# A five-layer hybrid block on one core: the layers behind the attention run in two halves of the tokens, woven into each other, and the attention loop is unrolled

## The chip, the cores and the metric

The kernel runs on one core of one Trainium2 chip. A core has five engines that run at the same time, each with its own queue of instructions: TensorE (PE in the profile, its weight loads PEld), VectorE (DVE), ScalarE (ACT), GpSimd (POOL) and SyncE (SP), which here only starts DMAs. Every queue is executed in order: an instruction that waits on a semaphore holds up all that stands behind it on its engine. The metric is the device time in microseconds of one execution.

## The reference

The input is 8 images of 64 channels and 16x16 pixels, 2048 tokens of 64 channels behind the convolutions. All is float32. Abridged:

```python
x = conv_attention(x)              # L0: non-local block on pooled keys, batch norm
x = binary_conv(x)                 # L1: 3x3 and 1x1 convolutions of signs
x = x + attention8(layernorm(x))   # L2: 8 heads per image, softmax over 256 tokens
n = layernorm(x)
x = x + sum_e gate2[e] * (gelu(n @ W1[e] + b1[e]) @ W2[e] + b2[e])       # 8 experts
x = x + haar_attention(layernorm(x), W_Q, pinv(W_Q), W_V, W_O)          # L3
n = layernorm(x)
x = x + sum_e gate3[e] * ((silu(n @ w1[e]) * (n @ w2[e])) @ w3[e])       # 16 experts
```

The gates are a softmax over the experts of which only the two largest count. The Haar attention has rotary queries and keys, their norms, scores against block sums, a variance-scaled softmax, and value sums by block. The pseudo-inverse of W_Q is found by a Newton iteration of 24 steps, whose small matrix products are run between those of the L2 attention.

## The kernel before

**Tokens and tiles.** The tokens stand as 16 tiles of 128 (`T`, 128 partitions by 16 by 64), the stream that the layers add to. For the experts the normed tokens are turned and split into a high and a low part (`XS`), 4 chunks of 512 tokens. The engines' programs are written out by hand, one block each, and tied by counted semaphores.

**Front.** L0 and L1, then `layer_norm(0)` on VectorE over all 16 tiles (`bn_stats` per tile, small operations, a square root on ScalarE, `tensor_tensor` multiplications at L1495, `split_low` at L375), the transposes in `ln_pe` and `split_high` on ScalarE.

**Attention.** `attention_steps` runs 36 steps on each engine, a pair of heads each, software-pipelined over five engines; 24 of them (3 rounds of 8) stand in a hardware loop, `Fori`. In those 24 steps TensorE also does the Newton products (`newton_a` L887, `newton_b` L891 and L892, tiles of 64x64), VectorE `newton_y` and `newton_x`, and GpSimd `newton_z`. GpSimd scales each block of probabilities (L494). Once per round of the loop VectorE copies the Newton factors (L1567).

**Behind the attention, all 16 tiles at once.** `layer_norm(1)`, the gate logits (L793), `gate(0)`, then the gates are transposed (L804), copied to `gT` (L578), stored to DRAM, and loaded back as rows that all partitions share (L428, L437). The first expert layer is 32 chunks (8 experts by 4 chunks): two `hidden` products, a gelu (L713), the multiplication by the gate row on VectorE (L1622), an `output` product. Meanwhile GpSimd has split the weights of the second expert layer (`split_weights`, L450 and L452), then it is idle. Next the sums are turned back (L1188), `layer_norm(2)`, the Haar attention (`l3_pe`, `l3_vector`, `l3_pool`), `layer_norm(3)`, gate logits, `gate(1)`, and the way through DRAM again.

**Last layer.** 64 chunks (16 experts by 4): four `hidden` products (L999) into a pair of PSUM banks (three pairs in turn), silu on ScalarE (L721), the product of the two halves on VectorE (L1639), the multiplication by the gate row on GpSimd (L548), an `output` product (L1007, two instructions each). `hidden` runs six chunks ahead of `output`; eight `hid` buffers.

## Time and profile before

| | us |
|---|---|
| median of 3 runs | 449.83 (449.23 to 450.18) |
| profiled execution, whole time | 450.27 |
| its span, first to last instruction | 448.3 |
| start to the end of L1 | 0 to 50.4 |
| first norm | 50.4 to 61.8 |
| attention | 61.8 to 211.5 |
| norm, gates, gate rows | 211.5 to 243.8 |
| first expert layer (32 chunks) | 243.8 to 278.5 |
| turn, norm, Haar attention, norm, gates, gate rows | 278.5 to 347.9 |
| last expert layer (64 chunks) and store | 347.9 to 448.3 |

All steps below are placed in the profiled execution's span; some 2.0 us of its time lie outside the span.

### The profile page before, as it was taken

The page shows a single profiled execution, that of the slowest core. Times are in us where ns is not written, and L with a number is a line of the kernel's source. Part 1 is how long each engine was busy: PE and PEld are TensorE (multiplying, and loading weights), DVE is VectorE, ACT ScalarE, POOL GpSimd, SP SyncE. Part 2 cuts the span into 40 slices and gives each one's busy share as a digit, 9 for nine tenths or more (in the row PEclk, how much of TensorE's full clock was granted, in tenths as well). Part 3 has the DMA queues.
Part 4 walks back from the last instruction along what each step waited for, and adds up shares of the span by engine and source line. Part 5 has one row for each costly group of instructions (what it writes and reads, how often), then busy time and mean ns, then how long its engine had stood idle before and what let it go on. Part 6 is the DMA issues. An engine that isn't in the chain of part 4 may idle for free.

```text
span 448.3 us, 6934 instructions
## 1 busy us (share of the span) xinstructions
PE 369.8 (83%) x2147; PEld 237.7 (53%) x2147; DVE 292.5 (65%) x691; ACT 219.0 (49%) x545; POOL 191.2 (43%) x186
## 2 busy tenths in 40 slices
PE   4577279999999999997394999763476899999996
PEld 1462166777777777775271344532264355555552
DVE  2857967777787777774962565998994144444443
ACT  1434267777777777784341455532145233434332
POOL 4300035544555455452850000050100888888885
PEclk9867559999999999999656899867588899999999
DMA  7805000000000000000005980000002855444421
GB/s 230 172 0 189 0 0 2 1 2 2 0 0 0 0 0 0 0 2 1 1 0 174 320 258 4 1 0 2 0 1 76 311 187 188 153 164 155 187 94 48
DMA packets 16698, 32.81 MB, mean 73 GB/s; under 512 B 5728, under 2 KB 9504, under 8 KB 16672
## 3 DMA queue, kind: packets, MB, share of 16 engines
q1 hardware_dynamic: 16672, 32.49, 22.3%
q8 instruction: 13, 0.21, 0.2%
q14 instruction: 13, 0.11, 0.1%
HBM read 31.76 MB, written 0.72 MB: 72 GB/s over the span
## 4 chain that ended last, share of the span: by engine, by line
PE 62%; DVE 21%; ACT 7%; issue 5%; DMA 2%; POOL 1%; POOLq 0%; SPq 0%; DVEq 0%; ACTq 0%
PE ps L999 13%; PE ps L1007 7%; PE ps L843 7%; PE ps L854 6%; PE ps L870 6%; PE ps L958 4%; PE ps L950 3%; DVE xn L1495 2%; ACT va_vb L607 2%; DVE ln L1477 2%; DVE XS L375 2%; PE ps L819 1%; PE ps L820 1%; DVE negmax L1547 1%; PE ps L891 1%
## 5 line engine op out<-in xcount | busy, mean ns | idle before, releaser
L494 POOL TENSOR_TENSOR va_vb<-va_vb,rowinv 128x512 f32<-128x512 f32 x64 | 67.1, 1049 | 74.4 <-DVE rowinv L1554 74.4
L999 PE MATMUL ps<-XS,w3hl 128*128 128x512 f32 x256 | 70.0, 417 | 0.7 <-ACT gT L578 0.7
L721 ACT ACTIVATE wy<-ps 128x512 f32<-128x512 f32 x64 | 38.2, 598 | 63.8 <-PE ps L999 63.8
L999 PEld LDWEIGHTS ps<-XS,w3hl 128*128 128x128 f32 x256 | 47.1, 194 | 34.5 <-DVE hid_more L1639 5.7
L607 ACT ACTIVATE va_vb<-ps,negmax 128x256 f32<-128x256 f32 x128 | 59.5, 472 | 10.7 <-DVE negmax L1547 10.3
L1547 DVE TENSOR_REDUCE negmax<-ps 128x2 f32<-128x512 f32 x64 | 44.1, 689 | 10.0 <-PE ps L843 9.0
L843 PE MATMUL ps<-keys_gates,xcur 128*128 128x256 f32 x256 | 48.0, 311 | 2.2 <-DVE keys_gates L1539 2.2
L458 POOL TENSOR_TENSOR xn<-T,lnc 128x512 f32<-128x512 f32 x4 | 4.2, 1042 | 101.3 <-DVE lnc L1485 101.3
L843 PEld LDWEIGHTS ps<-keys_gates,xcur 128*128 128x128 f32 x256 | 35.7, 195 | 14.7 <-issue 8.1
L854 PE MATMUL ps<-consts,va_vb 128*128 128x128 f32 x256 | 40.5, 280 | 2.8 <-POOL va_vb L494 2.4
L870 PE MATMUL ps<-pT,vproj 128*64 128x256 f32 x256 | 34.5, 392 | 0.0
L854 PEld LDWEIGHTS ps<-consts,va_vb 128*128 128x128 f32 x256 | 28.5, 142 | 9.2 <-POOL va_vb L494 4.5
L598 ACT ACTIVATE keys_gates<-ps 128x512 fp32r<-128x512 f32 x32 | 19.1, 598 | 26.9 <-PE ps L820 26.7
L607 ACT ACTIVATION_READ_ACCUMULATOR va_vb<-ps,negmax 128x1 f32 x128 | 25.7, 201 | 0.0
L1639 DVE TENSOR_TENSOR hid_more<-ps,wy 128x512 f32<-128x512 f32 x16 | 11.1, 692 | 20.6 <-ACT wy L721 20.6
L1539 DVE TENSOR_TENSOR keys_gates<-ps,keys_gates 128x512 fp32r<-128x512 f32 x32 | 21.9, 685 | 1.5 <-ACT keys_gates L598 1.4
L591 DVE COPY pT<-ps 128x512 f32<-128x512 f32 x32 | 21.6, 675 | 1.9 <-PE ps L854 1.9
L950 PE MATMUL ps<-XS,w2hl 128*128 128x512 f32 x64 | 22.3, 480 | 0.0
L780 PE MATMUL ps<-consts,xn 128*128 128x128 f32 x32 | 7.6, 369 | 17.4 <-DVE xn L1495 17.4
L1639 DVE TENSOR_TENSOR hid_g<-ps,wy 128x512 f32<-128x512 f32 x16 | 11.1, 692 | 14.8 <-ACT wy L721 14.8
L950 PEld LDWEIGHTS ps<-XS,w2hl 128*128 128x128 f32 x64 | 12.9, 222 | 14.2 <-issue 3.2
L1554 DVE RECIPROCAL rowinv<-rowsum 128x2 f32<-128x2 f32 x64 | 10.5, 165 | 15.1 <-ACT va_vb L607 14.4
(305 smaller groups left out, 749.0 us busy)
## 6 DMA issues: line engine op xcount, KB each, us to landing
pT<-gates_row SPq DMA_DIRECT2D x18, 512.0 KB, 4.7
vproj<-gates_row SPq DMA_DIRECT2D x16, 512.0 KB, 4.8
gate_row_keys<-gates_row SPq DMA_DIRECT2D x14, 512.0 KB, 4.7
early<-in_f_in SPq DMA_DIRECT2D x1, 2048.0 KB, 8.9
consts<-in_consts SPq DMA_DIRECT2D x1, 816.0 KB, 5.5
x<-in_x SPq DMA_DIRECT2D x1, 512.0 KB, 3.7
w2raw<-in_f_in SPq DMA_DIRECT2D x1, 512.0 KB, 3.8
out<-in_f_out SPq DMA_DIRECT2D x1, 512.0 KB
```

Source lines behind the costliest of these rows:

```text
L494: gp.tensor_tensor(prob[:, n % 4], prob[:, n % 4], rowinv[:, n % 4, :].unsqueeze(2).broadcast_to([P, U, N]), ALU.mult).then_inc(S("p_scale ...
L607: ins = act.activation(prob[:, n % 4, u, :], ps[:, 1 + n % 2, u * N:(u + 1) * N], ACT.Exp, bias=negmax[:, n % 4, u:u + 1], accum_out=rowsu ...
L721: act.activation(act_out[:, kk % 2, :], ps[:, 2 * (kk % 3), :], ACT.Silu).then_inc(S("f3_act"), 1)
L843: mm = pe.matmul(ps[:, 1 + n % 2, u * N:(u + 1) * N], xcur[:, g, u * P:(u + 1) * P], K[:, k % 2, n % 2, :], start=(part == 0), stop=(part ...
L854: mm = pe.transpose(ps[:, 3 + n % 2, su * N + u * P:su * N + (u + 1) * P], prob[:, n % 4, u, su * P:(su + 1) * P], ident)
L870: mm = pe.matmul(ps[h * C:(h + 1) * C, 5, 0:N], vproj[:, g, su, head * C:(head + 1) * C], pT[:, (2 * k + h) % 4, su, :], start=(k % 4 == 0 ...
L950: mm = pe.matmul(ps[:, kk % 4, :], w2hl[:, s, e], XS[:, c * CHUNK:(c + 1) * CHUNK], start=(s == 0), stop=(s == 1))
L999: mm = pe.matmul(ps[:, 2 * (kk % 3) + w, :], w3hl[:, s, e, w * HID:(w + 1) * HID], XS[:, c * CHUNK:(c + 1) * CHUNK], start=(s == 0), stop= ...
L1007: pe.matmul(ps[half, bank, :], out3[:, e, :], hid[kk % 8], start=False, stop=False, skip_group_check=True).then_inc(S("f3_out_chunk"), 1)
L1539: tt(KL[:, k % 2].rearrange("p h n -> p (h n)"), ps[:, 0, :], KH[:, k % 2].rearrange("p h n -> p (h n)").bitcast(F32), ALU.subtract).then_ ...
L1547: dve.tensor_reduce(negmax[:, n % 4, :], ps[:, 1 + n % 2, :].rearrange("p (u n) -> p u n", u=U), AX.X, ALU.max, negate=True).then_inc(S("m ...
L1639: tt(hid[kk % 8], ps[:, 2 * (kk % 3) + 1, :], act_out[:, kk % 2, :], ALU.mult).then_inc(S("f3_glu"), 1)
```

## The change

The order of the work behind the attention and the shares of the engines are new; the arithmetic is that of before, but for Newton's scale factors.

- Norms, gates and Haar attention take half the tokens (8 tiles) at a time. `NORMS` gives their order: norm 0 of both halves, norm 1 of both, then norms 2 and 3 of half 0, then 2 and 3 of half 1.
- `in_turn` and `chain_first` interleave two generators in each engine's program: a main one with a yield per chunk (per pair for TensorE, two yields) and a chain one. The Haar attention, norm 3 and gates of half 0 are woven into the first expert layer's half 1; those of half 1 into the last layer's half 0. The last layer's half 1 stands alone.
- Norm 0 of half 1 is done inside the first attention steps; norm 1 and the gates of half 0 inside the last ones; norm 1 and the gates of half 1 inside the first expert layer's half 0.
- GpSimd now multiplies by the gate rows in both expert layers; it splits the last layer's weights in 32 pieces, one in each of the first 32 attention steps.
- The attention is unrolled; Newton's copies of factors are gone; its products are 128 by 128 wide (`nsX` and `nsY` doubled).
- The norm's subtraction and multiplication are one `tensor_scalar` per tile. The copies of V3 move from VectorE to ScalarE. PSUM for hidden products is five single banks in turn (before: four banks, and three pairs), so that bank 5 is the Haar attention's.
- `keep_clock` (20 filler products on TensorE) is no longer called. Gate rows lie in eight slots of half the tokens.

```diff
+        def in_turn(main, chain, lead=0):
+            for k, _ in enumerate(main):
+                if k >= lead:
+                    next(chain, None)
+            for _ in chain:
+                pass
+        def chain_first(main, chain):
+            next(chain, None)
+            for _ in main:
+                next(chain, None)
+            for _ in chain:
+                pass
...
-            for k in range(-2, 2):
-                step(0, k, lambda pair: pair >= 0)
-            with eng.Fori(0, J - 1) as j:
...
+            for k in range(-2, STEPS + 2):
+                step(0, k, lambda pair: 0 <= pair < STEPS)
+                if beside:
+                    beside(k)
...
 # GpSimd
+        def weigh_pool(gp, which, h):
+            for k in range(2 * EXPERTS[which]):
+                K = 2 * EXPERTS[which] * h + k
+                slot, filled = row_of(which, h, k // 2)
+                gp.wait_ge(S(f"gate_row{slot}"), 16 * filled)
+                gp.wait_ge(S(("f2_act", "f3_glu")[which - 2]), K + 1)
+                gp.tensor_tensor(hid[K % 8], hid[K % 8], gate_rows[slot][:, k % 2 * CHUNK:(k % 2 + 1) * CHUNK],
+                                 ALU.mult).then_inc(S(f"f{which}_hid_ready"), 1)
+                yield
...
+            for _ in weigh_pool(gp, 2, 0):
+                pass
+            in_turn(weigh_pool(gp, 2, 1), chain_pool(gp, 0), lead=2)
+            in_turn(weigh_pool(gp, 3, 0), chain_pool(gp, 1), lead=5)
+            for _ in weigh_pool(gp, 3, 1):
+                pass
...
 # ScalarE
+            gT_act(act, 2, 0)
+            in_turn(gelu_act(act, 0), second_norm_act(act))
+            sums_act(act, 0)
+            ln_act(act, 2, 0, ACT.Gelu)
+            ln_high_act(act, 2, 0)
+            in_turn(gelu_act(act, 1), chain_act(act, 0, ACT.Gelu), lead=2)
+            sums_act(act, 1)
+            ln_act(act, 2, 1, ACT.Silu)
+            ln_high_act(act, 2, 1)
+            in_turn(silu_act(act, 0), chain_act(act, 1, ACT.Silu), lead=5)
+            for h in range(2):
+                if h == 1:
+                    for _ in silu_act(act, 1):
+                        pass
+                act.wait_ge(S("f3_out_chunk"), 2 * EXP3 * (h + 1))
+                act.activation(yfin[:, h, :], ps[:, 6 + h, :], ACT.Copy).then_inc(S("out_ready"), 1)
...
 # ScalarE, in chain_act
+            act.wait_ge(S("a_var_ready"), h + 1)
+            act.activation(s9[:, 3], s9[:, 2], ACT.Sqrt).then_inc(S("a_std_ready"), 1)
+            act.preload_act_table((ACT.Exp, table)[h])
+            yield
+            act.wait_ge(S("z_ready"), h + 1)
+            act.activation(e9[:], z9[:], ACT.Exp).then_inc(S("e9_ready"), 1)
+            act.preload_act_table((ACT.Sqrt, table)[h])
...
 # TensorE
+            gates_pe(pe, 2, 0)
+            in_turn(ffn2_pe(pe, 0), second_norm_pe(pe))
+            second = ffn2_pe(pe, 1)
+            next(second)
+            turn_pe(pe, 0)
+            ln_pe(pe, 2, 0)
+            chain_first(second, chain_pe(pe, 0))
+            pe.wait_ge(S("w3_split"), EXP3)
+            third = ffn3_pe(pe, 0)
+            next(third)
+            turn_pe(pe, 1)
+            ln_pe(pe, 2, 1)
+            chain_first(third, chain_pe(pe, 1))
+            for _ in ffn3_pe(pe, 1):
+                pass
...
+            def newton_a(s):
+                pe.wait_ge(S("nsx_ready"), s + 2)
+                pe.matmul(ps[:, 6, 0:C], as_weights(nsAT[:]), nsX[:, 2, :], start=True,
+                           stop=True).then_inc(S("ns_ax"), 1)
...
 # VectorE
+                for q in range(tiles.start, tiles.stop):
+                    ins = ts(xn[:, q, :], T[:, q, :], lnc[:, 1, q:q + 1], lnc[:, 7, q:q + 1], ALU.subtract, ALU.mult)
...
+            def chain(h):
+                for _ in range(4):
+                    yield
+                yield from l3_vector(dve, h, step, tt, ts, stt)
+                yield from layer_norm(3, h)
+                yield
+                yield from gate(3, h)
+            def products(h):
+                for k in range(2 * EXP3):
+                    K = 2 * EXP3 * h + k
+                    dve.wait_ge(S("f3_act"), K + 1)
+                    if K >= 8:
+                        dve.wait_ge(S("f3_out_chunk"), K - 7)
+                    tt(hid[K % 8], ps[:, (2 * K + 1) % 5, :], act_out[:, K % 2, :],
+                       ALU.mult).then_inc(S("f3_glu"), 1)
+                    yield
...
+            for h in range(2):
+                turn(h)
+                for _ in layer_norm(2, h):
+                    pass
+                if h == 0:
+                    for _ in chain(0):
+                        pass
+            in_turn(products(0), chain(1), lead=5)
+            for _ in products(1):
+                pass
```

`l3_vector` now has a yield behind each of its parts: squares' sums; two cosine products; rotation, norms and scaled basis; diagonal scores; scale; far scores; variance; standardised scores; exponentials' sums; diagonal weights; prefix part. `layer_norm` has four, `gate` two.

## Rows read from the trace of the kernel before

**Rows 1.** The page, busy time of each engine over the span (microseconds, share, instructions)
```profile
PE 369.8 (83%) x2147; PEld 237.7 (53%) x2147; DVE 292.5 (65%) x691; ACT 219.0 (49%) x545; POOL 191.2 (43%) x186
```

**Rows 2.** Busy time by stage: stretch, its length, engines' busy time, granted clock, DMA
```profile
50.40:61.80 11.40, 3.19 (x12) 2.45 (x12) 10.73 (x39) 5.13 (x11) 3.59 (x3) 0.50 0.00 0
61.80:211.50 149.70, 146.39 (x1102) 112.27 (x1102) 109.28 (x257) 108.33 (x344) 73.07 (x88) 0.98 0.00 1
211.50:243.80 32.30, 18.70 (x140) 13.40 (x140) 20.00 (x63) 10.86 (x21) 15.43 (x9) 0.63 0.11 31
243.80:278.50 34.70, 33.86 (x117) 13.24 (x118) 20.79 (x33) 17.16 (x27) 0.00 (x0) 0.90 0.66 216
278.50:288.10 9.60, 6.94 (x36) 3.43 (x36) 8.53 (x34) 3.51 (x7) 1.04 (x1) 1.00 0.01 2
288.10:323.00 34.90, 17.17 (x129) 11.21 (x129) 31.18 (x65) 10.59 (x30) 7.77 (x5) 0.65 0.00 1
323.00:338.50 15.50, 12.30 (x113) 9.82 (x114) 14.00 (x62) 6.86 (x14) 1.04 (x1) 0.72 0.01 1
...
347.90:448.30 100.40, 95.58 (x360) 48.58 (x360) 40.83 (x59) 35.30 (x59) 80.82 (x64) 0.98 0.46 164
```

**Rows 3.** The chain that ended last, the gates' way through DRAM: start, length, what
```profile
237.22 2.32 DMA gates_row<-gT
239.56 4.22 DMA pT<-gates_row
243.80 0.70 DVE hid_al L1622
```

**Rows 4.** Timeline, norm behind the attention: start, length, engine, line; GpSimd at work beside
```profile
216.99 7.00 DVE L1495 TENSOR_TENSOR xn<-xn,lnc 128x256 f32<-128x256 f32 x4
217.64 2.40 POOL L452 TENSOR_TENSOR w3hl<-early,w3hl 128x1024 fp32r<-128x1024 f32 x1
...
219.99 1.23 POOL L450 CAST w3hl<-early 128x1024 fp32r<-128x1024 f32 x1
...
221.30 2.40 POOL L452 TENSOR_TENSOR w3hl<-early,w3hl 128x1024 fp32r<-128x1024 f32 x1
```

**Rows 5.** Timeline, norm and Haar attention between the two expert layers
```profile
285.66 1.43 DVE L1495 TENSOR_TENSOR xn<-xn,lnc 128x256 f32<-128x256 f32 x4
...
313.28 0.31 DVE L1290 TENSOR_TENSOR t<-e,consts 128x144 f32<-128x144 f32 x1 [0.39 <-ACT e L757]
...
315.31 1.90 POOL L485 TENSOR_TENSOR x<-f_prob,pdia 128x1024 f32<-128x1024 f32 x1 [17.34 <-DVEq L1301]
315.33 2.03 DVE L1302 TENSOR_TENSOR t<-e,consts 128x128 f32<-128x128 f32 x1 [0.16 <-DVE pdia L1299]
```

**Rows 6.** The chain that ended last, one pair of chunks of the last expert layer
```profile
354.91 1.01 PE ps L1007 x4
355.92 2.07 PE ps L999 x8
```

**Rows 7.** Groups of instructions by line: busy us, mean ns, idle before
```profile
L721 ACT ACTIVATE wy<-ps 128x512 f32<-128x512 f32 x64 | 38.2, 598 | 63.8 <-PE ps L999 63.8
...
L1639 DVE TENSOR_TENSOR hid_more<-ps,wy 128x512 f32<-128x512 f32 x16 | 11.1, 692 | 20.6 <-ACT wy L721 20.6
...
L548 POOL TENSOR_TENSOR x<-x,pT 128x512 f32<-128x512 f32 x6 | 7.6, 1290 | 1.6 <-DVE x L1639 1.6
...
L564 ACT ACT_TABLE_LOAD x3 | 3.8, 1283 | 0.1
```

**Rows 8.** Timeline of TensorE, an attention step with Newton products, and one without
```profile
182.35 0.28 PE L820 MATMUL ps<-xcur,AL 128*128 128x256 f32 x1
...
183.22 0.72 PE L843 MATMUL ps<-keys_gates,xcur 128*128 128x256 f32 x4
...
187.03 0.28 PE L820 MATMUL ps<-xcur,AL 128*128 128x256 f32 x1
...
187.51 0.72 PE L843 MATMUL ps<-keys_gates,xcur 128*128 128x256 f32 x4
```

More of the change, by code:

```diff
@@ L14 @@
 from contextlib import ExitStack
+import itertools
 import math
@@ L439, in _ @@
-            for half in range(2):
-                sp.wait_ge(S(("out_ready_act", "out_ready_vec")[half]), 1)
-                s = slice(half * 512, (half + 1) * 512)
-                sp.dma_start(out[:, s], yfin[:, s]).then_inc(S("stored"), 16)
+                    slot, _ = row_of(which, h, e)
+                    if (which, h) == (2, 0) and e == 2:
+                        sp.wait_ge(S("pv_done"), PAIRS + STEPS)
+                    if (which, h) == (2, 1):
+                        sp.wait_ge(S("f2_hid_ready"), 2 * e + 2)
@@ new lines, in gate_pe @@
+        def gate_pe(pe, which, h):
+            experts, weight = {2: (EXP2, gw2), 3: (EXP3, gw3)}[which]
+            pe.wait_ge(S("gate_loaded"), 64)
+            pe.wait_ge(S("ln_low"), norm(which - 1 if which == 2 else 3, h) + 1)
+            for q in range(HT * h, HT * h + HT):
+                for o in range(2):
+                    tokens = slice(q * P + o * C, q * P + (o + 1) * C)
+                    mm = pe.matmul(ps[o * C:(o + 1) * C, 6 + h, (q % 8) * experts:(q % 8 + 1) * experts],
+                                   XS[:, tokens].bitcast(F32), weight[:], start=True, stop=True)
+            mm.then_inc(S("gate_logits"), 1)
@@ L961, in ffn2_pe, with output @@
-            pe.wait_ge(S("w2_split"), 1)
-            for kk in range(4):
-                hidden(kk)
-            gates_pe(pe, 0)
-            for kk in range(4, 6):
-                hidden(kk)
+            def output(k):
+                K, half = first + k, slice(C * (k % 2), C * (k % 2) + C)
+                pe.wait_ge(S("f2_hid_ready"), K + 1)
+                pe.matmul(ps[half, 6 + h, :], out2[:, k // 2, 0:C], hid[K % 8], start=False,
+                          stop=False, skip_group_check=True).then_inc(S("f2_out_chunk"), 1)
@@ L997, in hidden, with ffn3_pe @@
+            for k in range(0, 2 * EXP2, 2):
+                output(k)
+                output(k + 1)
+                yield
+                for kk in (k + 5, k + 6):
+                    if kk < 2 * EXP2:
+                        hidden(kk)
+                yield
+        def ffn3_pe(pe, h):
+            first = 2 * EXP3 * h
+            def hidden(k):
+                K, c = first + k, 2 * h + k % 2
                 for w in range(2):
+                    i = 2 * K + w
+                    if i >= 5:
+                        pe.wait_ge(S(("f3_act", "f3_glu")[(i - 5) % 2]), (i - 5) // 2 + 1)
@@ L1501, in gate @@
[L1501 to L1512 removed]
+                yield
@@ new lines, in layer_norm @@
+                step(ts(lnc[:, 1, tiles], lnc[:, 0, tiles], 0.5, None, ALU.mult))
+                yield
+                dve.wait_ge(S("ln_std"), i + 1)
+                step(dve.reciprocal(lnc[:, 7, tiles], lnc[:, 6, tiles]))
+                for q in range(tiles.start, tiles.stop):
+                    ins = ts(xn[:, q, :], T[:, q, :], lnc[:, 1, q:q + 1], lnc[:, 7, q:q + 1], ALU.subtract, ALU.mult)
+                    if q % 4 == 3:
+                        ins.then_inc(S("ln_normalised"), 1)
@@ new lines, in layer_norm, with gate @@
+                yield
+                split_low(dve, i)
+                yield
+            def gate(which, h):
+                g, q, bank = gating(which, h), half_tiles(h), 6 + h
+                experts, gb = {2: (EXP2, gb2), 3: (EXP3, gb3)}[which]
+                dve.wait_ge(S("gate_loaded"), 64)
+                lg, ge, gs = logit[:, q, 0:experts], gexp[:, q, 0:experts], gsel[:, q, 0:experts]
+                dve.wait_ge(S("gate_logits"), g + 1)
+                raw = ps[:, bank, 0:HT * experts].rearrange("p (t e) -> p t e", e=experts)
+                step(tt(lg, raw, gb[:].unsqueeze(1).broadcast_to([P, HT, experts]), ALU.add))
+                for t in range(q.start, q.stop):
+                    ins = dve.max(top8[:, t, :], logit[:, t, 0:experts])
```

1053 lines of the change are left out of this document (546 added, 507 removed).

## The prediction

> **What bounds the kernel now.** First the page's busy times: TensorE works 83% of the span, VectorE 65%, GpSimd 43% [rows 1]; no engine is full, so the stages must be read one by one. In the table of stages [rows 2] TensorE is busy 146.4 of 149.7 us of the attention, 33.9 of 34.7 of the first expert layer, 95.6 of 100.4 of the last. Between them nothing is full but VectorE: 31.2 of 34.9 us in the Haar attention, 14.0 of 15.5 in the norm and gates behind it, and TensorE's clock falls to 0.63 to 0.72. Third, the chain that ended last shows how the gates go through DRAM, 2.32 us to store and 4.22 to load [rows 3]. These serial stretches, 32.3 us behind the attention and 69.4 between the expert layers, are what there is to hide.
>
> Fourth, the timeline shows a coupling of two engines that this change will press on. Four VectorE multiplications, both inputs in SBUF, take 7.00 us while GpSimd runs its own back to back [rows 4], and 1.43 us with GpSimd idle [rows 5]: each of the four waits for the end of one GpSimd instruction. A 128x128 product takes 2.03 us beside a GpSimd one of 1.90, where one of 128x144 takes 0.31 alone [rows 5]. The products of the last layer, with one input in PSUM, keep 692 ns with GpSimd 81% busy [rows 2, 7]: they don't wait.
>
> **Start and attention.** Half a norm saves half of the work before the first scores: of 11.4 us [rows 2] some 2.8. The other half's VectorE work, about 5 us, goes into the filling of the pipeline, where each step waits for VectorE; I keep 1 us. Newton: `newton_a` lengthens a step by 0.39 us (L820 to L843 takes 0.87 with it, 0.48 without [rows 8]); the four transposes inside that 0.48 cost about 0.09 each, so two full-width instructions of a product cost about 0.2 (an estimate): 0.2 us less in 24 steps would be 5. `newton_b` gets one product twice as wide, no gain, and VectorE some 0.13 us more a step; I take 3 us (0 to 5). Unrolling removes 3 copies of factors: nothing, TensorE covers them. GpSimd is busy 73 of 149.7 us, so 32 pieces of weight splitting fit. Norm 1 of half 0 and its gates enter the last steps, some 6 us of VectorE work and its waits for GpSimd's scaling, where VectorE is three quarters busy (109.3 of 149.7 [rows 2]): plus 2. **Sum -2** (-5 to +3). The splitting stood beside other work before, so its move saves only the waits of rows 4.
>
> **Gates behind the attention.** Once T is complete (211.5) there remain for half 0 the gate operations on 8 tiles, 1.3 us up to the exponential, 0.4 for that and 1.1 behind it, transposes 0.6, copy 0.6, hand-offs 1 (estimates at the prices per operation below), then issue, store and load, 0.9 + 2.32 + 4.22 = 7.4 [rows 3]: 12.4 instead of 32.3. **-20** (-23 to -15).
>
> **First expert layer and chain of half 0.** Before: 243.8 to 347.9, 104.1 us. The weighing moves from VectorE (0.69 us) to GpSimd, which needs 1.29 us a chunk [rows 7]; TensorE needs 34.7/32 = 1.08. GpSimd becomes the bound: half 0 takes 16 x 1.29 = 20.6, plus 3 for a cold clock and the other half's norm: 24. Now ScalarE's program has the sums, the norm's root and `ln_high` of half 0 ahead of the next gelu, so all chunks stop for a half-size turn and norm: of the 9.6 us of before [rows 2] 9 remain, since bn_stats halve but the hand-offs don't. Then the chain of half 0: VectorE's own work in the two stretches of the chain was 31.2 + 14.0 = 45.2 us. Less about 4 of waits for GpSimd (1.7 in the last row of rows 5 alone), 2.5 of the previous norm's end and 2.3 of V3 copies, all estimates, leaves 36.4 in about 110 operations. An operation costs about 0.16 plus 1.04 ns an element (0.31 at 144, about 0.69 at 512); the elements halve, most of the fixed part stays: 23 us. Squares come 7 us after the start, hand-offs cost 4, and beside the 16 weighings about 12 locked operations wait 1.2 us each, 14: chain 48 us (40 to 55). The experts' 16 chunks, 20.6 us, hide in it. Then ScalarE again has sums, root and `ln_high` of half 1 ahead of the first silu, and TensorE two chunks of hidden products, 2 to 4 us, ahead of the turn: 11.5 us, which cover the gate rows of 7.4. 24 + 9 + 48 + 11.5 = 92.5, **-11.6** (-22 to -2).
>
> **Last layer.** Before, a pair of chunks takes 1.01 + 2.07 = 3.08 us of TensorE [rows 6], 1.54 a chunk, and the stage 100.4. Half 0 now has the chain of half 1 in it, on VectorE one part behind each product. Up to the ninth product no part comes: nine chunks of 1.54 less two that are ready, 10.8, start of sums 1.3, four rounds of projections 2.7, and 2.7 for the low clock at first, 17.5 us. Then 19 products of 0.69, 13; own chain work 23; locks: the weighing of chunk K begins as its product ends, just when the part starts, and 14 of the parts hold operations with two inputs in SBUF, or a `tensor_scalar`, which I count alike. At most 14 x 1.29 = 18, less what reductions cover: 15 (5 to 18). ScalarE has root and exponential between silus: it waits for VectorE's part, loads the table of silu again (1.28 us [rows 7]) and then does the silu of 0.60 that VectorE's next product waits for. Four such places at some 1.8: 7 (2 to 9). TensorE waits once for the basis while VectorE's hidden products run out: 3. Last three chunks 3. Half 0: 17.5 + 13 + 23 + 15 + 7 + 3 + 3 = 81.5, not 49. Covered by none: VectorE itself is the bound here. Then ScalarE waits for all of half 0's outputs before the next silu, so nothing of half 1 runs ahead: last output 0.5, 32 chunks of 1.54, 49.3, start of sums 1.3, the last chunk's silu, product, weighing and output, 0.60 + 0.69 + 1.29 + 1.0, and copy and store 3.3: 58.0. 139.5 against 100.4: **+39.1** (+22 to +50).
>
> The Trainium skill, "SBUF — State Buffer", section "Who interferes with whom", says that the pair of ports which VectorE and GpSimd share is locked for a whole instruction, for a VectorE operation with two SBUF inputs beside a GpSimd one that reads SBUF, and that the order of issue decides who waits. Rows 4 and 5 agree on the first. By the second, parts with one such operation at their head would wait nothing, and 12 parts cost the whole 1.29, 15.5 us instead of my 15: the same sum.
>
> **DMA and other edits.** Gate rows are as many bytes; three more loads of 16 KB at the start stand ahead of the constants, which VectorE's softmax covers by microseconds. Eight slots load earlier than they are needed. `keep_clock` fills a stretch whose TensorE work is small: 0 (up to +2 when cold products follow).
>
> **Sum.** 448.3 - 2 - 20 - 11.6 + 39.1 = 453.8 of span, plus 2.0 outside gives 455.8 beside the profiled run's 450.27; that lies 0.4 above the median: 455.4, said as 455.
>
> **Rivals.**
> - *Forecast: VectorE bounds the woven half of the last layer; what is hidden is paid back.* 455, own range 451 to 465. Chance 0.46.
> - *Other side: the locks and ScalarE's waits overlap and the chain runs in VectorE's gaps.* VectorE has about 0.85 us free per chunk before. If a part finds GpSimd's weighing finished (GpSimd is late, or the part's reductions stand first), locks cost 5 and table waits 2: half 0 takes 66.5, and the chain of half 0 some 43: 435. It decides once the woven half stays under about 76 us, all else as summed. For it: 1.54 us of TensorE against 0.69 of VectorE a chunk. Against: rows 4, every one of four operations waited. 425 to 448.9; chance 0.34.
> - *Stalls pile up.* Every engine's order is fixed by yields; a late part holds silu, products, then five PSUM banks, and TensorE falls to its low level, as between the layers before (0.65) [rows 2]. At the low level a chunk takes 3.07, and 10 more us go in each woven stretch: 475. For it: four engines wait for each other in turn. Against: at such a rate TensorE is busy all the time, and the clock was 0.98 wherever it was. 466 to 480; chance 0.13.
> - *Gain and loss cancel* within 0.2% (0.9 us, about what a measurement of this kernel can tell from no change): 0.07.
>
> So: faster 0.34, same 0.07, slower 0.59. Range 432 to 472, over the other side's middle and into the pile-up.
>
> **What would show it.** First weighed chunk at about 222; next stop of GpSimd of 9 us near 246 to 255; first weighing of the last layer near 314 to 316; weighings of the woven half every 3 us or more from its ninth chunk, with SBUF products of VectorE ending just behind GpSimd's instructions; its end near 395; then 1.54 a chunk. I am wrong if the woven half's chunks go by at under 2.4 us, if the chain of half 0 ends before 295, or if `newton_a` didn't shorten.

## The result and the profile after

The changed kernel takes 523.03 us (median of 4 runs, 520.72 to 525.43) where the kernel before takes 449.66: 1.1634 times as long, 95% interval 1.1591 to 1.1676. The prediction was 455 us, range 432 to 472: slower, as said, but by 73 us and not by 5. The profiled execution's span went from 448.3 to 523.6 us (that execution, 525.43 us, is the longest of the four).

The page's busy times, and its rows of busy tenths and granted clock, each over the span in 40 slices:

```profile
PE 397.3 (76%) x2139; PEld 256.6 (49%) x2140; DVE 284.0 (54%) x751; ACT 252.9 (48%) x577; POOL 231.3 (44%) x241
...
PE   5772548999999999668766877544949195699997
...
DVE  3677567677667767743203174545376565424442
...
PEclk9756579999999999967968597556987656799999
```

VectorE is busy 284.0 us, less than before (292.5 [rows 1]), and falls from 65% to 54% of the span: the kernel did not get longer because VectorE has more to do. Table of stages, as [rows 2] (stretch, its length, busy time of each engine with instructions, granted clock, DMA share, GB/s):

```profile
60.50:233.60 173.10, 152.88 (x1142) 122.22 (x1142) 118.58 (x307) 114.45 (x353) 90.60 (x121) 0.94 0.01 1
233.60:245.30 11.70, 8.60 (x38) 5.95 (x38) 5.93 (x38) 7.54 (x10) 0.04 (x1) 0.63 0.29 85
245.30:279.90 34.60, 25.48 (x95) 9.62 (x95) 3.57 (x17) 11.87 (x18) 19.80 (x16) 0.85 0.42 152
279.90:290.50 10.60, 3.85 (x16) 2.44 (x17) 6.01 (x26) 5.57 (x8) 0.09 (x1) 0.82 0.52 211
290.50:352.30 61.80, 41.64 (x192) 21.16 (x193) 28.74 (x85) 29.52 (x50) 25.42 (x19) 0.67 0.00 1
352.30:363.80 11.50, 4.89 (x16) 3.11 (x15) 6.01 (x26) 5.87 (x9) 0.00 (x0) 0.65 0.53 211
363.80:471.10 107.30, 77.72 (x320) 44.91 (x321) 55.63 (x119) 38.35 (x68) 45.03 (x35) 0.75 0.25 90
471.10:523.60 52.50, 49.29 (x200) 26.09 (x199) 21.79 (x32) 19.09 (x32) 40.39 (x32) 1.00 0.30 105
```

The stages are the attention, the gates of half 0, first experts of half 0, turn and norm 2, the Haar chain of half 0 beside the first experts of half 1, turn and norm 2 again, the chain of half 1 beside the last experts of half 0, the last experts of half 1. Against the prediction, in us:

| term | predicted | measured | before to after |
|---|---|---|---|
| attention's end | -2 | 211.5 to 233.6 | +22.1 |
| gates to first weighing | 12.4 | 11.7 | -20.6 |
| first experts half 0 | 24 | 34.6 | |
| turn and norm 2 | 9 | 10.6 | |
| chain of half 0 | 48 | 61.8 | |
| turn and norm 2 | 11.5 | 11.5 | +14.4 for this row and the three above |
| last experts half 0 | 81.5 | 107.3 | |
| last experts half 1 | 58.0 | 52.5 | +59.4 for this row and the one above |

22.1 - 20.6 + 14.4 + 59.4 = 75.3 us, the whole difference of the spans. Every stretch in which two streams of work are woven is far over its price, and those that are not (11.7, 10.6, 11.5, 52.5) are at most 1.6 us over it (10.6 for 9). In the woven half of the last layer no engine is busy more than 77.7 of 107.3 us, and TensorE's clock is at 0.75, where the last half has 1.00.

**What a woven stretch looks like.** The waits of the changed kernel, TensorE in the woven half of the last layer (waiting instruction, what it waited for, us in total, times, longest):

```profile
PE ps L1247 <- DVE p L1459: 11.2, 1, 11.2
PE ps L1226 <- DVE pg_vsum L1402: 6.4, 1, 6.4
PE ps L916 <- DVE xn L1661: 6.1, 2, 5.8
PE ps L937 <- DVE gates L1688: 4.8, 1, 4.8
```

All four lines are waits for VectorE's part of the chain, 28.5 us. With the 77.7 us in which TensorE is busy they make 106.2 of the 107.3 us, so the length of this half is that of TensorE's queue with four stops in it. The longest, in the timeline of the three engines (start, length, engine, line, in brackets the idle time before it and what ended it):

```profile
403.20 1.28 ACT L795 ACT_TABLE_LOAD   x1
...
405.14 0.69 DVE L1811 TENSOR_TENSOR hid_more<-ps,wy 128x512 f32<-128x512 f32 x1
...
405.55 1.08 PE L1151 MATMUL ps<-x,out 128*64 128x512 f32 x4
...
406.01 1.32 DVE L1437 TENSOR_TENSOR t<-z 128x72 f32<-128x72 f32 x1
...
408.10 0.21 ACT L795 ACTIVATE s<-s 128x8 f32<-128x8 f32 x1 [3.62 <-DVE s L1440]
408.32 1.28 ACT L796 ACT_TABLE_LOAD   x1
409.62 0.60 ACT L742 ACTIVATE wy<-ps 128x512 f32<-128x512 f32 x1
...
410.23 1.28 ACT L799 ACT_TABLE_LOAD   x1
...
410.25 0.69 DVE L1811 TENSOR_TENSOR hid_al<-ps,wy 128x512 f32<-128x512 f32 x1 [2.18 <-ACT wy L742]
...
413.08 0.26 ACT L799 ACTIVATE e<-z 128x72 f32<-128x72 f32 x1 [1.57 <-DVE z L1448]
413.37 1.28 ACT L800 ACT_TABLE_LOAD   x1
414.66 0.60 ACT L742 ACTIVATE wy<-ps 128x512 f32<-128x512 f32 x1
...
415.29 0.69 DVE L1811 TENSOR_TENSOR hid_al<-ps,wy 128x512 f32<-128x512 f32 x1 [2.24 <-ACT wy L742]
...
415.90 0.22 DVE L1451 TENSOR_TENSOR t<-e,consts 128x72 f32<-128x72 f32 x1
...
417.51 0.23 DVE L1459 TENSOR_TENSOR p<-e,consts 128x64 f32<-128x64 f32 x1
...
417.79 0.48 PE L1247 MATMUL ps<-consts,p 128*128 128x128 f32 x1 [11.16 <-DVE p L1459]
```

Read it as a round, in which the activation tables that the loads switch belong to root, exponential and silu. ScalarE's root stands ahead of a silu whose input is ready, and waits 3.62 us for VectorE's variance. The silu follows at 409.62, behind a table load. VectorE's next part of the softmax stands behind the product of that silu, so it waits too; ScalarE's exponential then waits for that part, and so on. TensorE's transpose of `p` stands in its queue ahead of the hidden products and has to sit out two such rounds, so that for 11.16 us TensorE makes nothing for the experts either. Neither stream hides the other: each waits for the other's wait. In these 12 us only two chunks passed VectorE's product (at 410.25 and 415.29); at the pace of the last half (3.08 us a pair, the rows below, as [rows 6]) it would be eight. The chain that ended last of the changed kernel, last experts of half 1:

```profile
479.54 1.01 PE ps L1151 x4
480.55 2.07 PE ps L1144 x8
```

**The attention.** Its length is made of steps with Newton products (from the first `nsY` to the last) and of the filling and emptying around them. VectorE's waits in the Newton steps of the changed kernel (75 to 200 us):

```profile
DVE nsY L1736 <- POOL nsZ L543: 27.9, 24, 1.4
```

and the chain that ended last, in one of those steps (start, length, what):

```profile
130.94 1.04 POOL va_vb L535
131.98 0.69 POOL w3hl L565
132.68 0.26 POOL nsZ L543
132.94 0.03 issue
132.96 0.04 DVE nsY L1736
```

GpSimd scales the second block of probabilities (L535), then does a piece of the split of the layer 3 weights (L565), and only then makes `nsZ`, for which VectorE and behind it TensorE stand still. GpSimd is busy only 65.5 of the 110.0 us from the first `nsY` to the last, but its piece stands in the one place where somebody waits for what comes next. `newton_a` itself did get shorter: 0.65 us from its projections to the next scores, where it was 0.87.

The attention's +22.1 us in parts: it starts 1.3 us earlier; the filling is 7.9 longer (experiment 3); from there to the first `nsY` 1.9; the 23 periods between the first and the last `nsY` 3.4 (110.0 for 106.6); the emptying 10.2.

### The profile page after: what moved, and what is told of

Read it like the earlier page. It is cut to its first block, busy times and chain, and to the rows that moved or that the text cites. A ratio compares the mean times of both kernels' runs of the same rounds, so it can differ in the third digit from the quotient of the medians.

```text
span 523.6 us, 6763 instructions
## 1 busy us (share of the span) xinstructions
PE 397.3 (76%) x2139; PEld 256.6 (49%) x2140; DVE 284.0 (54%) x751; ACT 252.9 (48%) x577; POOL 231.3 (44%) x241
## 4 chain that ended last, share of the span: by engine, by line
PE 38%; DVE 26%; ACT 13%; POOL 11%; issue 10%; DMA 1%; POOLq 0%; DVEq 0%; SPq 0%; ACTq 0%
PE ps L1144 11%; POOL va_vb L535 5%; ACT va_vb L675 5%; PE ps L1151 4%; DVE negmax L1715 3%; PE ps L1103 3%; DVE xn L1661 3%; PE ps L1096 2%; DVE keys_gates L1707 2%; POOL w3hl L565 2%; PE ps L1002 1%; DVE rowinv L1722 1%; PE ps L1083 1%; DVE XS L413 1%; PE ps L975 1%
## 5 line engine op out<-in xcount | busy, mean ns | idle before, releaser
L535 POOL TENSOR_TENSOR va_vb<-va_vb,rowinv 128x512 f32<-128x512 f32 x64 | 66.7, 1042 | 80.2 <-DVE rowinv L1722 80.2
L1144 PE MATMUL ps<-XS,w3hl 128*128 128x512 f32 x256 | 76.4, 447 | 0.0
L1144 PEld LDWEIGHTS ps<-XS,w3hl 128*128 128x128 f32 x256 | 52.2, 214 | 30.0 <-issue 6.1
L578 POOL TENSOR_TENSOR hid_al<-hid_al,probT_rot 128x512 f32<-128x512 f32 x12 | 15.2, 1280 | 69.7 <-DVE hid_al L1811 39.7
L975 PEld LDWEIGHTS ps<-keys_gates,xcur 128*128 128x128 f32 x256 | 35.9, 197 | 18.2 <-issue 10.4
L1002 PE MATMUL ps<-pT,vproj 128*64 128x256 f32 x256 | 36.2, 407 | 0.0
L986 PEld LDWEIGHTS ps<-consts,va_vb 128*128 128x128 f32 x256 | 30.7, 149 | 8.7 <-POOL va_vb L535 6.9
L916 PE MATMUL ps<-consts,xn 128*128 128x128 f32 x32 | 9.7, 407 | 31.4 <-DVE xn L1661 31.2
L578 POOL TENSOR_TENSOR x<-x,row_keys 128x512 f32<-128x512 f32 x12 | 15.5, 1305 | 19.8 <-DVE x L1811 14.5
L578 POOL TENSOR_TENSOR hid_g<-hid_g,vproj 128x512 f32<-128x512 f32 x12 | 15.8, 1327 | 18.9 <-ACT hid_g L730 10.9
L1736 DVE SCALAR_TENSOR_TENSOR nsY<-ps,consts,nsZ 128x128 f32<-128x128 f32 x24 | 8.4, 351 | 27.9 <-POOL nsZ L543 27.9
L1811 DVE TENSOR_TENSOR hid_al<-ps,wy 128x512 f32<-128x512 f32 x16 | 11.0, 691 | 22.3 <-ACT wy L742 22.2
```

Source lines behind the costliest of these rows:

```text
L535: gp.tensor_tensor(prob[:, n % 4], prob[:, n % 4], rowinv[:, n % 4, :].unsqueeze(2).broadcast_to([P, U, N]), ALU.mult).then_inc(S("p_scale ...
L578: gp.tensor_tensor(hid[K % 8], hid[K % 8], gate_rows[slot][:, k % 2 * CHUNK:(k % 2 + 1) * CHUNK], ALU.mult).then_inc(S(f"f{which}_hid_read ...
L975: mm = pe.matmul(ps[:, 1 + n % 2, u * N:(u + 1) * N], xcur[:, g, u * P:(u + 1) * P], K[:, k % 2, n % 2, :], start=(part == 0), stop=(part ...
L986: mm = pe.transpose(ps[:, 3 + n % 2, su * N + u * P:su * N + (u + 1) * P], prob[:, n % 4, u, su * P:(su + 1) * P], ident)
L1002: mm = pe.matmul(ps[h * C:(h + 1) * C, 5, 0:N], vproj[:, g, su, head * C:(head + 1) * C], pT[:, (2 * k + h) % 4, su, :], start=(k % 4 == 0 ...
L1144: mm = pe.matmul(ps[:, i % 5, :], w3hl[:, s, k // 2, w * HID:(w + 1) * HID], XS[:, c * CHUNK:(c + 1) * CHUNK], start=(s == 0), stop=(s == 1))
```

## The experiments

Twelve kernels ran. All times are medians of the device time; the changed kernel's 523.0 is the reference for those built from it, and the ratio is to the kernel before with its 95% interval. The kernel before, timed beside each group of runs, took 449.7 to 450.7 us, so a difference of about 1 us between kernels of different groups is nothing. Lengths of stages come from one profiled execution each, which lies up to 4.4 us from its kernel's median; a difference of 2 or 3 us between stages of two kernels is within that.

**1. Only the unrolling.** The kernel before, with

```diff
-            with eng.Fori(0, J - 1) as j:
+            for j in map(Round, range(J - 1)):
```

> The kernel before, with the hardware loop over the rounds of the attention written out and nothing else of the change. If unrolling in itself is neutral and the 22 us that the attention lost come from what was woven into it, this stays within 2 us of the kernel before (448 to 452 us). If straight-line code itself costs the engines time (fetching instructions that a loop would have kept), the attention grows here too and the time is 460 to 472 us.

449.65 us, ratio 1.0007 (0.9985 to 1.0030). Unrolling is neutral; the attention's loss is in what was put into it.

**2. The scaled identity a step earlier.** The changed kernel, with

```diff
-                if s > 0:
-                    gp.wait_ge(S("nsy_ready"), s)
-                gp.tensor_tensor(nsZ[:], ...
+                if s > 1:
+                    gp.wait_ge(S("nsy_ready"), s - 1)
+                gp.tensor_tensor(nsZ[:, s % 2], ...
...
-                    newton_z(newton_at(k))
+                    newton_z(newton_at(k + 1))
```

> The changed kernel with two buffers for the scaled identity of the Newton steps, made one step earlier on GpSimd. In the changed kernel VectorE waits 27.9 us for it, 24 times. If that wait sets the length of a Newton step (4.78 us), the step falls to the 4.6 us or less and the time by 3 to 8 us (515 to 520 us). If it is only the last of several waits on a step that something else sets, the wait moves to the TensorE product or to GpSimd's scaling and the time stays within 1.5 us of 523.

514.87 us, ratio 1.1473 (1.1415 to 1.1530): 8.2 us less. The 23 periods between the first and last `nsY` take 102.4 us, not 110.0: 4.45 us each instead of 4.78. In this kernel VectorE waits for nothing of GpSimd in them. That is also 4.2 us under the kernel before (106.6).

**3. Nothing beside the attention.** The norm's second half ahead of the attention, norm 1 and gates of half 0 behind it, on all engines:

```diff
             ln_pe(pe, 0, 0)
+            ln_pe(pe, 0, 1)
+            pe.wait_ge(S("ln_low"), 2)
             attention_pe(pe)
+            pe.wait_ge(S("qkvw_ready"), 6)
+            ln_pe(pe, 1, 0)
+            gate_pe(pe, 2, 0)
```

> The changed kernel with the first norm's second half put ahead of the attention and the norm and gates of half 0 put behind it, so that nothing of them stands inside the attention. Theory: inserted work stops the pipeline while it fills and drains; the attention itself gets 12 to 16 us shorter, and the moved work costs about 4 us ahead and 12 to 14 us behind, so that the sum is near zero (519 to 528 us). Rival: the inserted work was hidden and the attention is longer for another reason (unrolling, GpSimd's pieces); then the attention is not shorter by more than 3 us and the time rises by 14 to 18 us (537 to 541 us).

522.06 us, ratio 1.1588 (1.1546 to 1.1630): no change that can be told. Stages of this kernel, the filling (first scores to first products) and the emptying (last `nsY` to the last `add_out`), then the same two of the changed kernel and of the kernel before:

```profile
67.80:79.00 11.20, 10.48 (x58) 8.13 (x58) 6.39 (x14) 7.96 (x27) 4.50 (x5) 0.83 0.00 1
195.20:223.00 27.80, 25.13 (x192) 18.70 (x191) 17.85 (x43) 19.52 (x62) 16.30 (x19) 1.00 0.01 1
```

```profile
60.50:79.60 19.10, 12.02 (x61) 10.01 (x61) 11.91 (x37) 12.11 (x32) 4.53 (x5) 0.71 0.00 0
195.00:233.60 38.60, 31.25 (x228) 22.63 (x227) 25.03 (x68) 22.52 (x66) 16.34 (x20) 0.89 0.00 1
```

```profile
61.80:73.00 11.20, 10.58 (x58) 8.52 (x58) 6.39 (x14) 8.09 (x27) 4.16 (x4) 0.79 0.00 1
183.10:211.50 28.40, 26.05 (x202) 19.53 (x200) 17.62 (x40) 20.53 (x65) 12.47 (x12) 1.00 0.00 1
```

With nothing inserted, filling and emptying have their old lengths. Inserted, they get 7.9 and 10.2 us longer (19.1 for 11.2, 38.6 for 28.4), which is what the same work costs when it stands in the open: 7.3 us ahead of the attention (60.5 to 67.8), and 9.4 behind it (21.1 from its end to the first weighing instead of 11.7). The weaving hid nothing of it. In the filling TensorE waits 6.9 us for the normed tiles while ScalarE's root with its two table loads holds up the next keys.

**4. The chain of half 1 by itself.** The changed kernel, the same on each engine:

```diff
-            in_turn(products(0), chain(1), lead=5)
+            for _ in itertools.chain(chain(1), products(0)):
+                pass
```

> The changed kernel with the Haar attention, norm and gates of half 1 run whole, ahead of the last experts of half 0, on all engines. Theory: a half's chain is a line of dependent short steps and takes about 50 us by itself, no less than both halves took together; then experts take their clean 55 us: 105 to 110 us where the woven stretch took 103, and the time is 525 to 532 us. Rival: the weaving itself makes the stalls (mutual waits of engines in order, locks between VectorE and GpSimd, table loads), and unwoven the chain takes 38 to 42 us: the stretch shrinks to 90 to 97 us and the time to 509 to 517 us.

508.61 us, ratio 1.1317 (1.1288 to 1.1346): 14.4 us less. The chain alone and then the experts of half 0, stages of this kernel:

```profile
357.90:400.50 42.60, 18.90 (x114) 13.28 (x115) 24.99 (x87) 21.14 (x36) 3.54 (x3) 0.50 0.15 61
400.50:451.60 51.10, 50.92 (x204) 27.61 (x203) 22.04 (x32) 19.64 (x34) 40.44 (x32) 0.99 0.49 165
```

One after the other they take 93.7 us; woven, the same stretch (from the copy of norm 2's transposes on) takes 109.3. My first theory fell, its rival stands: the weaving makes the stalls. VectorE's instructions of `l3_vector` take 16.4 us here and 24.6 in the changed kernel, those of `layer_norm(3, 1)` 5.4 and 7.3 (durations of the single instructions, summed).

**5. and 6. The other two weavings undone.** Norm 1 and gates of half 1 behind the first experts of half 0 on TensorE and ScalarE; then, in a kernel of its own, the chain of half 0 behind the first experts of half 1 on all engines:

```diff
-            in_turn(ffn2_pe(pe, 0), second_norm_pe(pe))
+            for _ in itertools.chain(ffn2_pe(pe, 0), second_norm_pe(pe)):
+                pass
```

```diff
-            chain_first(second, chain_pe(pe, 0))
+            for _ in itertools.chain(second, chain_pe(pe, 0)):
+                pass
```

> The changed kernel with norm 1 and the gates of half 1 behind the layer 2 experts of half 0 on ScalarE and TensorE, in place of woven among them (VectorE's order is unchanged). The woven stretch took 34.6 us from the first weighing to the sums' copy. Theory that weaving makes the engines wait for each other in order: the experts alone take 20 to 24 us and the norm and gates behind them 10 to 14 us, so the sum is within 3 us of the changed kernel (520 to 526 us) although nothing overlaps any more. Rival, that weaving hid the norm: the time rises by its 10 to 14 us (533 to 537 us).

> The changed kernel with the chain of half 0 (Haar attention, norm 3, gates 3) behind the layer 2 experts of half 1 on all engines. Woven, the two took 62 us. With the 42 us that the chain of half 1 took alone and 24 us for 16 expert chunks, the theory that this weaving gains nothing gives 64 to 68 us and 524 to 529 us in all. If this weaving costs as much as the one in the last layer did, 510 to 517 us; if it really hid the experts, 535 us and more.

518.82 us, ratio 1.1521 (1.1468 to 1.1575), 4.2 us less; and 521.02 us, ratio 1.1525 (1.1454 to 1.1596), 2.0 us less, its interval just overlaps that of the changed kernel. The first is under both of its ranges, the second between the first two of its three. In the profiles the attention's end to the copy of half 0's sums takes 41.5 us in experiment 5, for 46.3 in the changed kernel; from that copy to that of half 1's sums experiment 6 takes 69.8 us, for 72.8. Neither weaving gained anything. The first lost some 4 us; of the second no loss is shown.

**7. No table changes.** The changed kernel with Copy or Identity in place of these roots and exponentials, and no `preload_act_table`:

```diff
-            act.activation(s9[:, 3], s9[:, 2], ACT.Sqrt).then_inc(S("a_std_ready"), 1)
-            act.preload_act_table((ACT.Exp, table)[h])
+            act.activation(s9[:, 3], s9[:, 2], ACT.Copy).then_inc(S("a_std_ready"), 1)
```

> The changed kernel with every square root and exponential behind the attention's end (but those of norm 1 and the gates of half 0) replaced on ScalarE by Copy or Identity, so that no table changes between the chain and the Gelu or Silu of the experts. It leaves out those roots and exponentials; every instruction but the loads stays. The trace of the changed kernel has 28 such loads from 235 us on, 1.28 us each, 35.8 us. If they stand on the path because ScalarE's order ties chain and experts together, the time falls by 20 to 35 us (488 to 503 us). If most lie in time in which ScalarE would wait anyway, by 4 to 12 us (511 to 519 us).

512.46 us, ratio 1.1383 (1.1364 to 1.1401): 10.6 us less, for 28 loads and 35.8 us of ScalarE. Seven tenths of the loads' time were not on the path, as its second range said. The woven half of the last layer falls from 109.3 to 102.9 us, and is still 9 us longer than the two in sequence with all their loads. The round of waits stays without the loads, ScalarE's timeline of this kernel:

```profile
396.58 0.21 ACT L797 ACTIVATE s<-s 128x8 f32<-128x8 f32 x1 [4.70 <-DVE s L1440]
396.70 0.58 ACT L745 ACTIVATE wy<-ps 128x512 f32<-128x512 f32 x1
400.15 0.35 ACT L800 ACTIVATE e<-z,eps_ln 128x72 f32<-128x72 f32 x1 [2.87 <-DVE z L1448]
400.41 0.58 ACT L745 ACTIVATE wy<-ps 128x512 f32<-128x512 f32 x1
```

**8. Weighing on VectorE in the woven stretches,** so that GpSimd has almost nothing beside the chain:

```diff
                        ALU.mult).then_inc(S("f3_glu"), 1)
+                    if h == 0 and k >= 1:
+                        weigh_vector(3, K - 1, k - 1)
```

> The changed kernel with the weighing of the experts' outputs on VectorE in the two woven stretches (layer 2 half 1, layer 3 half 0), as layer 2 had it before, so that GpSimd is idle beside VectorE's chain. In the changed kernel the chain's two-input VectorE instructions took 38 us beside GpSimd's weighing in the last layer and 27.4 us alone. If these locks matter on the path, the time falls by 8 to 15 us (508 to 515 us) in spite of 48 more instructions of 0.6 us on VectorE. If the waits in order matter and VectorE has slack, it stays within 3 us; if VectorE's own work is the bound, it rises by 10 to 25 us (533 to 548 us).

518.66 us, ratio 1.1504 (1.1465 to 1.1543): 4.4 us less, between its first range and its second. The locks are gone, `l3_vector` takes 15.5 us and not 24.6, the norm 5.3 and not 7.3. Of these 11 us the stretch gave back at most 2.8 (109.3 to 106.5, within what two profiles differ by), while VectorE has 8 us of work more in it (64.9 against 57.0). VectorE's own time is not what sets its length.

**9. Everything behind the attention in sequence,** with experiment 2's edit:

> The changed kernel with nothing woven behind the attention any more (second norm, chain of half 0 and chain of half 1 each run by themselves) and the scaled identity one Newton step ahead: the four changes that were each tried alone together. If their savings are of separate stretches they add up: 523 less 14.4, 8.2, 4.2 and 2 to 4, that is 492 to 496 us. What then stands above the kernel before (about 44 us) is the price of halving alone. If the waits only move from one stretch to another, 500 us and more.

496.51 us, ratio 1.1030 (1.0986 to 1.1075). 26.5 us less, near the 28.8 of the four alone (14.4, 8.2, 4.2 and 2.0), and half a microsecond over its first range. Two stages of it, the chain of half 0 and that of half 1:

```profile
295.40:336.80 41.40, 19.95 (x121) 11.53 (x121) 23.61 (x85) 16.11 (x31) 6.65 (x6) 0.64 0.00 1
...
347.00:388.40 41.40, 17.70 (x112) 12.07 (x113) 24.99 (x87) 20.72 (x36) 3.54 (x3) 0.54 0.15 56
```

Each takes 41.4 us, where both halves at once took 34.9 + 15.5 = 50.4 [rows 2]. Of the 46.1 us that the span is still longer than before's, 2 x 41.4 - 50.4 = 32.4 are this, 12.3 the attention's later end, 5.2 the other norms and experts between (81.8 against 76.6), and -3.8 the last layer (106.0 against 109.8 from the end of the chain on).

Why a half costs 41.4 us shows in the same rows. VectorE is busy 23.6 + 25.0 = 48.6 of the 82.8 us, about what it was for both halves at once (31.2 + 14.0 = 45.2 of 50.4): its work did halve, and its waits went from 5.2 us to 34.2. ScalarE is busy 36.8 us instead of 17.5, and 17 loads of activation tables (7 and 10, 1.28 us each) stand in the two stretches, where the chain of both halves at once had 4. These are 16.7 us more of loads; how many of them VectorE waited for was not measured.

**10. The same edit of the Newton step in the kernel before,** on top of experiment 1:

> The kernel before, its attention's rounds written out, with two buffers for the Newton step's scaled identity, made a step ahead, and its factors read straight from the table of constants. In the kernel before VectorE waited only 5.9 us for GpSimd there, in 24 steps of 4.67 us. If that wait is on the path, the steps fall to 4.45 us as they did in the changed kernel with the same edit, and the time by 3 to 6 us (444 to 447 us), faster than both kernels. If the step is set by the TensorE and VectorE exchange alone, the time stays within 1.5 us of 450.

448.87 us (12 runs; before 450.22 in 17), ratio 0.9972 (0.9955 to 0.9988). That is 0.3% under the kernel before, and within the 1.5 us of its second range: the 23 periods take 106.2 us against 106.6, so the wait for GpSimd was hardly on the path there. It had been 5.9 us in all. It is gone, and VectorE's waits for the scores went from 7.6 us to 12.4:

```profile
DVE negmax L1554 <- PE ps L850: 12.4, 24, 0.7
```

**11. VectorE's load without the chain's waits.** Experiment 4's kernel, with

```diff
                        ALU.mult).then_inc(S("f3_glu"), 1)
+                    if h == 0:
+                        step(tt(m_a, m_b, m_c, ALU.mult))
```

> The kernel in which the chain of half 1 runs by itself, ahead of the experts of half 0 (508.6 us, its 32 chunks in 51.1 us), with one more VectorE instruction of 128x512, two inputs in SBUF, behind each product of half 0: as much VectorE work as the chain has (it had 27 us alone, 38 us beside GpSimd), but bound to nothing on other engines. The results are not used. If it was VectorE's load and its locks with GpSimd that stretched the woven experts to 109 us, the stretch grows here by 25 us and more (535 us). If it was the waits of the chain for other engines, VectorE's work fits beside the experts: 51 to 62 us for the stretch and 509 to 520 us in all.

515.00 us, ratio 1.1462 (1.1414 to 1.1510). The experts of half 0 with that load, and the added instruction in the groups by line:

```profile
399.90:457.70 57.80, 55.40 (x204) 26.79 (x203) 52.46 (x64) 19.75 (x34) 53.98 (x32) 0.99 0.42 145
```

```profile
L1817 DVE TENSOR_TENSOR va_vb<-va_vb 128x512 f32<-128x512 f32 x32 | 33.0, 1031 | 0.0
```

VectorE has 52.5 us of work, as much as in the woven half of the changed kernel (55.6), GpSimd waits for it and it for GpSimd, and the 32 chunks take 57.8 us, not 107.3. TensorE keeps a clock of 0.99. The added load costs 6.7 us (51.1 to 57.8). Not in this kernel's stretch are the chain's instructions on TensorE (18.9 us by themselves at a clock of 0.50 in experiment 4, so some 9.5 at the full one) and on ScalarE, which has time for them. Were all of TensorE's added, the stretch would take 67 to 77 us. The other 30 to 40 us up to 107.3 are what a load on VectorE doesn't explain. TensorE's own four waits are 28.5 of the woven half. The clock has a share too: TensorE's work in that half was 77.7 us at a clock of 0.75, while the same work is 50.9 us for the experts at 0.99 and 9.5 for the chain at the full clock, 60.4. So some 17 us of the woven half are the lower clock (an estimate from these rows), and no experiment takes it apart from the waits: in experiments 4 and 11, where TensorE hardly waited, the experts ran at 0.99.

**12. The weight pieces out of the attention.** The changed kernel with GpSimd's 32 pieces behind the attention instead of in it:

```diff
             attention_steps(gp, step, beside)
+            split_weights(gp, w3hl, w3raw, [slice(e, e + 1) for e in range(EXP3)], "w3_loaded", "w3_high", "w3_split")
```

> The changed kernel with GpSimd's 32 pieces of the layer 3 weights' split taken out of the attention's steps and put behind them, ahead of the first weighing. If these pieces are what makes the scaled identity of the Newton steps late, VectorE's wait for it (27.9 us in 24 steps) falls below 10 us and the steps shorten from 4.78 to 4.5 to 4.65 us, 3 to 7 us in all; the split then takes 18 us and more behind the attention, of which GpSimd's idle time up to the first weighing covers 8 to 12, so that the time is 520 to 530 us. If the wait stays above 20 us, the pieces are not its cause, and the time rises by the uncovered 8 us or more (531 us).

513.16 us, ratio 1.1403 (1.1368 to 1.1437): 9.9 us less; its range was 520 to 530. VectorE's wait in the Newton steps:

```profile
DVE nsY L1727 <- POOL nsZ L543: 7.6, 23, 0.6
```

The 23 periods take 102.8 us (4.47 each). The attention's emptying is 37.0 us from the last `nsY` for 38.6; in experiment 2, which leaves the pieces in it, it is 37.8, so little of that is the pieces'. The 18.2 us of pieces fit into GpSimd's idle time up to the first weighing almost whole: that comes 12.4 us behind the attention's end instead of 11.7.

## Why the prediction was wrong

**Right.** The gates' way (11.7 us for 12.4), the turn and norm 2 (10.6 and 11.5 for 9 and 11.5) and that they stay long, and the unwoven last half (52.5 for 58; 1.54 a chunk, as said). Unrolling at nothing (experiment 1). `newton_a` shorter by 0.2 us, and the Newton periods 4.2 us shorter in all for 3 (0 to 5), once GpSimd wasn't late in them (experiment 2). The locks in size: 15 us (5 to 18), measured 8.2 + 1.9 in chain and norm, of which the time gave back less (experiment 8). The 7 us for ScalarE's places come near the 6.4 of experiment 7, but by luck: I counted four places, and the half has 10 table loads.

**Where it failed, the last layer.** The step is the sentence "Covered by none: VectorE itself is the bound here". VectorE's load was about right: 13 + 23 + 15 and the first nine products, some 57 us, and it was busy for 55.6. What failed is that its line sets the length. Measured were 107.3 us, in which TensorE was busy for 77.7 and waited 28.5 for VectorE's chain, where I had one wait of 3; and its work took some 17 us more for the lower clock, where I had 2.7. Experiment 11 puts the like of VectorE's work beside the experts, locks included, and they take 57.8 us, 67 to 77 with the chain's TensorE work: the bound by load lies there, and 30 to 40 us come from the waits in order and the lower clock beside them.

In the chain of half 0 (61.8 us for 48) VectorE was no bound either, busy for 28.7. The 48 us had the 16 chunks of experts hidden, and nothing was hidden: in sequence (experiment 6) the same work took no longer. The first experts (34.6 us for 24) show in experiment 5: there the 16 chunks alone take 21.1 us from the first weighing (243.99) to the last output product (265.06), about the 20.6 of the sum, and norm and gates of the other half 8.8 behind them in the open. Woven, both took 34.6, 4.7 more than one after the other; of the norm, which the sum had hidden but for some of 3 us, nothing was.

**Where it failed, the attention.** "GpSimd is busy 73 of 149.7 us, so 32 pieces of weight splitting fit" argued from a share of busy time. The pieces cost 7.2 to 7.6 us in the Newton steps (experiments 12 and 2) because they stand ahead of `nsZ`, and that ate the 4.2 us that the new Newton products gave. And "plus 2" for the tail and a saving of 1 at the start: the insertions lengthened filling and emptying by 7.9 and 10.2 us (experiment 3), as much as the work costs in the open. Perhaps because the pipeline has no second pair in flight there to cover a wait; no run shows that. Together +22.1 instead of -2.

**The rivals.** "Stalls pile up" named the mechanism, in-order waits with TensorE falling to its low level, and got 0.13 and 466 to 480 us. What I held against it, "at such a rate TensorE is busy all the time", was false: it was busy 77.7 of 107.3 us, at a clock of 0.75. I priced it at 10 us a woven stretch; the last layer alone was 25.8 over its sum. The other side, that the chain would run in VectorE's gaps, held for the load alone (experiment 11) and not for the chain. Two of my three signs of being wrong looked for a faster kernel, and none for stalls.

**What halving itself costs** was only half in the sum. I had the chain of a half at 48 us beside experts and compared that with the experts it would hide. Experiment 9 shows the floor: 41.4 us for a half against 50.4 for both. The instruction of 72 elements above (L1451) takes 0.22 us, its like of 144 took 0.31 [rows 5], and the waits and table loads of the chain don't halve but are paid twice. For the change to win, the weaving had to hide more than 46 us; behind the attention it cost 18 (514.9 of experiment 2 against 496.5 of experiment 9).

**Left open.** Whether a weaving with more distance between a part and the part that waits for it would gain was not tried. Experiments 5, 7 and 8 change the clock's course as well as the waits; what part of their few us is the clock's was not separated. Nor were `keep_clock`, the five single PSUM banks and the first experts' weighing on GpSimd tried by themselves. That the order of waits makes the stalls rests on experiments 4 and 11 and on the trace of the last layer's woven half.

## What to carry to other kernels

Before weaving two streams on in-order engines, write down for each inserted instruction that waits what stands behind it, and what the thing it waits for is standing behind: where two engines each hold the other's next input behind their own wait, the streams can run slower than one after the other (here 109.3 us for 93.7), however idle the engines look. Price the load by itself (here 6.7 us) and the waits by themselves (here 30 to 40, the lower clock with them). Put filler work where nobody waits for the next instruction of that engine (behind the attention 32 pieces cost 1 us, inside it over 7), and halve a chain of dependent short steps only if the second half is truly hidden, since here a half cost 82% of the whole.

## What the runs showed of the hardware

- A table load took 1.28 us and the next activation began at once: the load at 408.32 ends at 409.60, the silu starts at 409.62. The Trainium skill, page "ScalarE: Activation LUTs", section "What ACT_TABLE_LOAD costs", adds 1380 ns of drain to its 1283 ns. The trace agrees on the load; in these rows no such drain follows it, and none stands ahead of it either (the root ends at 408.31, the load starts at 408.32).
- `tensor_scalar` with two per-partition operands is also held up by GpSimd: eight of 128x64 take 1.9 us alone (experiment 4) and 2.9 beside the weighing (changed kernel). The whole difference is in one of the eight: it takes 1.31 us, the weighing that begins in the same moment (436.78) 1.26, and the others take 0.30 as alone:

```profile
L1664 DVE TENSOR_SCALAR xn<-T,lnc 128x64 f32<-128x64 f32 x8 | 1.9, 309 | 0.0
```

```profile
L1661 DVE TENSOR_SCALAR xn<-T,lnc 128x64 f32<-128x64 f32 x8 | 2.9, 429 | 0.0
```

- Locks work both ways: in experiment 11 one weighing of GpSimd takes 1.73 us on average, against 1.29 in experiment 4, without VectorE's added instruction, which itself takes 1.03.
